# Attention heads turned by VectorE in 32x32 blocks and by transfers that exchange blocks, in place of TensorE

## What is computed

```python
for l in range(3):                       # first network, one head
    scores = leaky(si[:, :, None] + sj[:, None, :] + attn_b[l])
    attn = softmax(where(mask, scores, -inf))
    h = layernorm(x + attn @ x, g1[l], beta1[l])
    x = layernorm(h + gelu(h @ W1[l] + b1[l]) @ W2[l] + b2[l], g2[l], beta2[l])
x = layernorm(x0 + x)
xp = x @ W_proj                          # second network, 8 heads
scores = leaky(a_src[:, :, :, None] + a_dst[:, :, None, :] + b_att)
att = softmax(where(A > 0, scores, -1e30))
x = layernorm(x + relu(att @ xh))        # xh: xp by heads
```

## Time and profile before

| | us |
|---|---|
| median of 3 runs | 2389.0 (2386.5 to 2389.7) |
| the profiled execution | 2386.6 |
| its span, first to last instruction | 2384.8 |
| start, to the first unit | 52.4 |
| pair 0 | 241.7 |
| each pair from 2 to 6 | 281.0 |
| tail, from the last unit's first product | 176.3 |

### The profile page before, as it was taken

The page is one execution under the profiler, slowest core; times in us unless marked ns, Lnnn a source line. Parts: engine busy times, 40 slices in busy tenths (PEclk is TensorE's granted clock), DMA queues, the critical chain, the costliest instruction groups (busy, mean ns, idle before and its releaser), DMA issues.

```text
span 2384.8 us, 33626 instructions
## 1 busy us (share of the span) xinstructions
PE 2285.7 (96%) x11169; PEld 1629.3 (68%) x11169; DVE 1715.9 (72%) x5676; ACT 1775.3 (74%) x3415; POOL 168.0 (7%) x200
## 2 busy tenths in 40 slices
PE   3999999999999999999999999999999999999866
PEld 2667667767776776777677777767776776777543
DVE  5455886588767877678766787668867687767587
ACT  2444478877888778887787878887788877888786
POOL 0000100000000000000000000000100000000000
PEclk9999999999999999999999999999999999999977
DMA  6011021022111132011320121210211111200011
GB/s 214 10 36 36 33 96 61 20 67 89 44 55 49 34 105 63 22 50 37 97 72 23 67 85 27 76 50 32 93 42 54 54 36 63 67 19 23 31 44 33
DMA packets 85783, 131.56 MB, mean 55 GB/s; under 512 B 4424, under 2 KB 53868, under 8 KB 85612
## 3 DMA queue, kind: packets, MB, share of 16 engines
q1 hardware_dynamic: 85612, 129.41, 16.7%
HBM read 120.74 MB, written 8.65 MB: 54 GB/s over the span
## 4 chain that ended last, share of the span: by engine, by line
PE 86%; DVE 6%; ACT 6%; issue 1%; DMA 0%; POOL 0%; SPq 0%; POOLq 0%; DVEq 0%; ACTq 0%
PE ffn L1116 25%; PE av L1041 13%; PE ffn L1105 12%; PE av L1105 12%; PE pT L1024 12%; PE av L1057 5%; ACT prob L459 2%; PE av L1092 2%; PE av L1140 1%; PE trow L1140 1%; DVE prob L703 1%; ACT prob L453 1%; PE trow L1003 1%; DVE prob L694 1%; ACT l1x L493 1%
## 5 line engine op out<-in xcount | busy, mean ns | idle before, releaser
L1116 PE MATMUL ffn<-w_sb,G 128*128 128x256 f32 x3072 | 752.5, 381 | 0.9 <-ACT G L477 0.9
L1116 PEld LDWEIGHTS ffn<-w_sb,G 128*128 128x128 f32 x3072 | 553.5, 191 | 77.9 <-issue 14.2
L1024 PEld LDWEIGHTS pT<-ident,prob 128*128 128x128 f32 x2816 | 356.2, 145 | 207.1 <-issue 121.5
L703 DVE CUSTOM_DVE_ANT_0 prob<-trow,mask 128x512 f32<-128x512 f32 x704 | 458.3, 686 | 38.8 <-PE av L1065 16.9
L1024 PE MATMUL pT<-ident,prob 128*128 128x128 f32 x2816 | 440.1, 282 | 45.9 <-DVE prob L748 16.1
L459 ACT ACTIVATE prob<-prob,nm 128x512 f32<-128x512 f32 x512 | 362.8, 711 | 0.0
L453 ACT ACTIVATE prob<-prob,s 128x512 f32<-128x512 f32 x512 | 349.2, 714 | 9.1 <-DVE nm L710 7.7
L1105 PE MATMUL ffn<-hT,w_sb 128*128 128x512 f32 x768 | 354.9, 595 | 1.1 <-ACT hT L472 1.1
L1105 PE MATMUL av<-hT,w_sb 128*128 128x512 f32 x768 | 353.3, 592 | 0.0
L468 ACT COPY prob<-pT 128x512 f32<-128x512 f32 x452 | 260.7, 581 | 101.8 <-PE pT L1024 100.3
L409 POOL TENSOR_TENSOR rstd<-veps,mhalf 128x4 f32<-128x4 f32 x127 | 152.6, 1202 | 2175.6 <-DVE veps L638 2175.6
(11 more groups left out here) (119 smaller groups left out, 2468.2 us busy)
## 6 DMA issues: line engine op xcount, KB each, us to landing
w_sb<-in_L_gnn_W SPq DMA_DIRECT2D x48, 1024.0 KB, 8.4
trow<-rows_dram SPq DMA_DIRECT2D x128, 256.0 KB, 3.2
adj_sb<-in_adj SPq DMA_DIRECT2D x16, 1024.0 KB, 5.5
xin<-in_x SPq DMA_DIRECT2D x16, 512.0 KB, 6.3
x0r<-in_x SPq DMA_DIRECT2D x16, 512.0 KB, 4.5
out<-o SPq DMA_DIRECT2D x15, 512.0 KB, 3.0
aw_row<-in_L_gnn_attn_w SPq DMA_DIRECT2D x1, 768.0 KB
g_row<-in_L_gnn_g SPq DMA_DIRECT2D x2, 384.0 KB
```

The source lines that it names most:

```text
L703: return v.tensor_tensor_reduce(out=out_[:, t, :], in0=targets, in1=mask[:, t, :], scale=1.0, scalar=LEAST, op0=ALU.add, op1=ALU.max, accu ...
L1024: last = te.transpose(pT[bank][:, j * P:(j + 1) * P], src[:, t, j * P:(j + 1) * P], ident[:])
L1116: last = te.matmul(ffn[part][:, at:at + D], G[:, f, t * P:(t + 1) * P], w2_sb[:, g // 2 % STAGES, f, :], start=f == 0, stop=f == FT - 1)
```

## The change

Heads 0 to 101 are no longer turned by TensorE. `turn_blocks` on VectorE transposes each 32x32 block of a head in one instruction over 128 x 2048 elements, from the ring buffer into a new buffer `blocks`, of which there is one. `move` on SyncE then copies it back into the ring in 16 transfers of 32 partitions by 2 KB (64 KB each) that put each group of 32 partitions where it belongs. VectorE waits before each turn for the transfers of the head before (`s_moved`), and TensorE before `attend_heads`. The moved heads have their columns in another order, so the product reads them through a wider pattern (`sources`). Heads from 102 on (`MOVED`, unit `BY_PE` = 44) are turned as before. The room for `blocks` comes from `y_att`, now a part of `prob0`, and from one row buffer less (`ROWS` = 2); VectorE therefore waits for the normalised state before it computes scores.

The order changes with it. The slots make 3, 3, 3, 3, 3, 1 heads. Four heads are attended (`spent_by`) in k0, k2 and k5 ahead of the second product's first pieces and in k3 behind the attention. A unit's second and third old heads are turned on VectorE before and after the attention, its own first head at its end. The bias sum moves behind the attention (`plus_bias`), the end of a graph from before the attention to behind it, with GpSimd's order following; the masks move from k4 to k2 (kept) and k3 (made), those in k5 stay.

```diff
-ROWS = 3
+ROWS = 2
+BLOCK = 32
+BLOCKS = P // BLOCK
-MADE_IN_SLOT = [3, 3, 3, 3, 2, 2]
-MADE_AT_LAST = [3, 3, 3, 3, 3, 1]
+MADE_IN_SLOT = [3, 3, 3, 3, 3, 1]
+BY_PE = UNITS - 4
+SPENT_IN_SLOT = [-SIDE, None, 0, SIDE, None, 2 * SIDE]
...
+MOVED = made(BY_PE)[0]
 def turned(g):
-    return made(g - 1) if g else []
+    return made(g - 1) if g > BY_PE else []
+def spent_by(g):
+    p, k = g // SLOTS - 1, g % SLOTS
+    if g > BY_PE or SPENT_IN_SLOT[k] is None:
+        return None, False
+    four = 2 * HEADS * p + SPENT_IN_SLOT[k]
+    return (four, k != 3) if four >= 0 else (None, False)
...
-        y_att = sb("y_att", [P, T, D])
+        y_att = prob0[:, :, 0:D]
+        blocks = sb("blocks", [P, BLOCKS, N])
...
+            def move(q):
+                sp.wait_ge(s_block, q + 1)
+                for a in range(BLOCKS):
+                    for b in range(BLOCKS):
+                        sp.dma_start(ring(q)[b * BLOCK:(b + 1) * BLOCK, a, :],
+                                     blocks[a * BLOCK:(a + 1) * BLOCK, b, :]).then_inc(s_moved, 16)
...
+            def turn_blocks(q):
+                dve.wait_ge(s_exp, T * (q + 1))
+                if q:
+                    dve.wait_ge(s_moved, 16 * BLOCKS * BLOCKS * q)
+                v.transpose(blocks[:].rearrange("p b (x i) -> p x b i", i=BLOCK),
+                            ring(q)[:].rearrange("p t (j b i) -> p (t j) b i", b=BLOCKS, i=BLOCK)).then_inc(s_block, 1)
...
+            def sources(q, j):
+                if q < MOVED:
+                    return ring(q)[:].rearrange("p a (t j i) -> p j t a i", t=T, j=T)[:, j]
+                return ring(q)[:, :, j * P:(j + 1) * P]
...
+                if q < MOVED:
+                    pe.wait_ge(s_moved, 16 * BLOCKS * BLOCKS * min(q + SIDE, MOVED))
...
                 if g:
                     layer_ends(1 - s, unit_of(g - 1)[2])
+                dve.wait_ge(s_hn, c("hn"))
...
                 for q in new[:1]:
                     head_maxima(q)
-                done = ended(g)
-                if done is not None:
-                    graph_sum(done)
                 if att:
-                    if ends is not None:
-                        first_network_ends(ends)
-                    attention(s2, l2, *new[1:2])
+                    if ends is not None:
+                        first_network_sum(ends)
+                        if ends % 2 == 0:
+                            first_network_ends(ends)
+                    if spent is not None and ahead:
+                        heads_out(spent)
+                    for q in old[1:2]:
+                        turn_blocks(q)
+                    attention(s2, l2, *new[1:2])
+                    for q in old[2:]:
+                        turn_blocks(q)
+                if done is not None:
+                    graph_sum(done)
+                if ends is not None and ends % 2:
+                    first_network_ends(ends)
                 if done is not None:
                     graph_out()
+                plus_bias(s, l)
                 if att:
                     fed_forward(s, 0)
-                if k >= SLOTS - 2:
-                    keep_masks(k - SLOTS + 2)
+                if k == 2:
+                    keep_masks(0)
+                if k == 3 and p < PAIRS - 1:
+                    make_masks(0)
+                if k == SLOTS - 1:
+                    keep_masks(1)
                     if p < PAIRS - 1:
-                        make_masks(k - SLOTS + 2)
+                        make_masks(1)
                 for q in new[2:]:
                     head_made(q)
                 if four is not None:
                     heads_out(four)
+                if spent is not None and not ahead:
+                    heads_out(spent)
+                if g < BY_PE:
+                    for q in new[:1]:
+                        turn_blocks(q)
```

More of the change, by code:

```diff
@@ L205, in targets_of @@
             if graph == GRAPHS - 1:
[L206 removed]
+                return prob0[0:HEADS, 0, :]
             return ring(room(graph))[0:HEADS, DT, :]
@@ L349, in _ @@
                 last = p == PAIRS - 1
-                new = made(g)
+                new, old = made(g), made(g - 1)
                 if k == 0 and not last:
@@ L360, in _ @@
                     load_rows(q + 1)
[L361 to L364, removed]
+                if g <= BY_PE:
+                    for q in old[1:2]:
+                        move(q)
                 if k == 0 and not last:
@@ L367, in _ @@
                     load_x(2 * p + 3)
+                for q in new[1:2]:
+                    load_rows(q + 1)
+                if g <= BY_PE:
+                    for q in old[2:]:
+                        move(q)
+                if ended(g) is not None:
+                    store_out(ended(g))
                 if k == SLOTS - 2 and not last:
@@ L427, in _ @@
                     inverse_deviation(ATTENDED)
+                if ended(g) is not None:
+                    inverse_deviation(LAST)
+                if first_ends(g) is not None and first_ends(g) % 2:
+                    inverse_deviation(RESIDUAL)
             inverse_deviation(FED)
@@ L531, in _ @@
                 place, four = side_by_side(heads)
+                spent, ahead = spent_by(g)
                 att = g + 1 < UNITS
@@ L584, in _ @@
                         head_rows(four)
+                    if t == 0 and spent is not None and not ahead:
+                        head_rows(spent)
                     if t == 1 and att:
@@ L918, in _ @@
                 att = g + 1 < UNITS
-                new = made(g)
+                new, old = made(g), made(g - 1) if 0 < g <= BY_PE else []
                 four = side_by_side(turned(g))[1]
-                ends = first_ends(g)
+                spent, ahead = spent_by(g)
+                ends, done = first_ends(g), ended(g)
                 if g:
                     layer_ends(1 - s, unit_of(g - 1)[2])
+                dve.wait_ge(s_hn, c("hn"))
+                dve.sem_inc(s_passed, 1)
                 if att:
@@ L1200, in _ @@
                             turn(q, f - T)
+                if four_spent is not None and ahead:
+                    attend_heads(four_spent)
                 for t in range(T):
                     piece(t)
+                    if t == 2 and four_spent is not None and ahead:
+                        heads_back(four_spent)
                 if att:
@@ L1225, in _ @@
                         attend_heads(four)
+                    if t == 0 and four_spent is not None and not ahead:
+                        attend_heads(four_spent)
                     if t == 1 and att:
@@ L1230, in _ @@
                         heads_back(four)
+                    if t == 2 and four_spent is not None and not ahead:
+                        heads_back(four_spent)
                 if place == 2:
```

52 lines of the change are left out of this document (32 added, 20 removed).

## The result

The changed kernel takes 2542.8 us (median, 2537.6 to 2547.1) against 2388.9 us, a ratio of 1.0645 (95% interval 1.0623 to 1.0667). The forecast was 2410 us within 2345 to 2470: the sign was right, the size was not, and the range ended 73 us too low. The profiled run, 2541.4 us, has a span of 2539.6 us.

What follows compares the result with a forecast made beforehand. TensorE bounded the kernel before (86% of the chain); afterwards VectorE would end last in five of six slots. Profiled 2386.6 - 6 (walk) + 25 (clock) + 3 (moves) = 2409, median 2.4 higher: 2410 us, range 2345 to 2470.

Steps and rivals of the forecast that it cites:

- The transpose: VectorE's new turn of one head, 128x2048 float32, taken at 2.25 us, the pace of the reduction; 36 us per pair.
- the cheap-transpose rival: VectorE's turns behind the attention cost only 1.23 us each, giving back 57 us: 2342 us; chance 0.13.
- VectorE's work: VectorE's busy time per pair of graphs rises from 209 by 36 to 245 us.
- The wider access pattern: TensorE's four-head product reads the moved heads through a wider pattern, costed at nothing.
- The walk: Step-by-step timing of the pair's six units, k0 to k5, summing to 281.4 us against 280.95; -6 us over the run.
- the clock: TensorE's idle gaps before the scores lower its granted clock, 0.85 us on average for 30 units: +25 us.
- the 28 us taken from TensorE: Dropped head turns free 28.1 us of TensorE per full pair, which come back as waiting for VectorE in five of six slots.
- the 252.5 us in the text: TensorE's busy time per pair after the change: 280.6 less 28.1 us for the turns removed.
- the price of an issue: Each SyncE transfer issue costs 0.30 to 0.43 us, so a head's sixteen-transfer move takes 7.3 to 10.1 us.
- the moves are late: Rival: at 0.6 us an issue a move takes 12.8 us, VectorE waits 12 us per pair: 2480 us; chance 0.17.
- The first row of a graph in k0: SyncE's row load behind the moves in slot k0, put at 12 us against 14 needed.
- moving masks and spent heads costs nothing by itself: Relocating mask work and four-head attention between slots levels the slots and by itself costs nothing.

Runs made afterwards that it cites:

- e1: Changed kernel without its transfers: VectorE still turns the heads' blocks, nothing is exchanged between partitions, products not the reference's; 2419.0 us, ratio 1.0118.
- e3: Changed kernel with 4 transfers per head instead of 16, same bytes, blocks keep their partitions, products not the reference's; 2417.6 us, ratio 1.0123.
- e5: The kernel of e3 with TensorE's gaps filled by 16 unread identity transposes in each unit behind one that made heads; 2439.9 us, ratio 1.0219.
- e8: Kernel before with only the changed kernel's storage (two row buffers, shared attended array), no head turned by VectorE; 2394.6 us, ratio 1.0028.
- e2: Changed kernel with the same 16 transfers per head, each carrying 32 KB instead of 64 KB, products not the reference's; 2533.6 us, ratio 1.0615.
- e10: Changed kernel with each head's 16 transfers shared by two queues, 8 issued by SyncE and 8 by GpSimd; 2551.5 us, ratio 1.0686.
- e4: Changed kernel with TensorE turning every head, no VectorE transposes or transfers, new order and storage kept except the four-head products' places; 2452.6 us, ratio 1.0269.

## Why the prediction was wrong

**The steps that held.** *The transpose*: 2310 ns against 2.25 us, so the cheap-transpose rival is out by its own row. It took the reduction's pace. *VectorE's work*: 246 us per pair against 245. *The wider access pattern*: a matmul of the four-head product takes 602 ns in both kernels, 114 us in all. *The walk.* VectorE's period from one second feed-forward sum to the next, mean of pairs 2 to 6, in us:

| slot | walk | e1 | e3 | after | of it waiting for moves |
|---|---|---|---|---|---|
| k0 | 48.4 | 49.5 | 49.8 | 49.5 | 0 |
| k1 | 42.1 | 43.3 | 43.0 | 50.1 | 8.47 |
| k2 | 48.1 | 48.3 | 48.4 | 51.9 | 3.95 |
| k3 | 47.8 | 48.7 | 48.7 | 50.0 | 1.95 |
| k4 | 46.1 | 46.5 | 46.9 | 49.6 | 2.49 |
| k5 | 48.9 | 49.9 | 49.6 | 54.2 | 4.16 |
| sum | 281.4 | 286.2 | 286.4 | 305.3 | 21.02 |

With moves absent (e1) or in time (e3), the sum lies 4.8 to 5.0 us above the walk; the clock's 0.85 us in five slots is 4.3 of that. So the waiting for VectorE that eats the 28 us taken from TensorE is there as forecast. *The clock's* size fits, though no run separates it: in e3, which has nothing else to slow them, the first layer's matmuls have means of 621 and 618 ns where the kernel before had 595 and 592; 768 x (26 + 26) ns is 40 us over 48 units, 0.83 us each. A granted clock of 0.97 over the 286 us of e3's pair is an estimated 17 us at the lower level, 3.4 us in each of five slots, about as long as the forecast's gap. One such gap in the kernel after, a stretch of 4 us in which TensorE worked for 1.1 us, and the stretch behind it (columns as above):

```profile
1258.00:1262.00 4.00, 1.09 (x7) 0.84 (x7) 3.92 (x18) 0.69 (x1) 0.00 (x0) 1.00 0.42 107
1262.00:1266.00 4.00, 4.00 (x7) 1.58 (x6) 3.72 (x12) 1.42 (x3) 0.00 (x0) 0.57 0.10 25
```

Behind the gap the granted clock is 0.57, close to the lower of the two levels, as in the earlier trace rows. Whether all of its cost lies on the path stays open, since e5 did not separate it. TensorE's busy time is longer than the 252.5 us in the text, too: 264 us per pair in e1 and e3 and 270 in the kernel after. In e3's pair some 7 of the 11 us lie in the first layer's matmuls.

**The step that failed: the price of an issue, and where its waits fall.** The text put an issue at 0.30 to 0.43 us, from the earlier trace rows, and a move at 7.3 to 10.1 us. It was 0.59 us in the median, 10.0 to 11.1 us for sixteen, 11.5 to 12.9 for a move. The rows taken were those of one small store and of broadcasts out of DRAM; no row of before showed an SBUF-to-SBUF transfer, and I took the cheap end although the same rows held 1.51 us for one weight load (one issue, not several, and no row shows that the queue was full, as the rival has it). The rival "the moves are late" had exactly this size, 0.6 us and 12.8 us, and still gave 2480: it counted 12 us of waiting per pair, and there are 21. It laid waits into k2 to k5 from the 10 us between the turns on either side of the attention, and none into k1, because k1 was TensorE's slot there. The shorter distance it left out: from the third old head's turn to the turn at the unit's end. k1 has neither masks nor spent heads there, so by the walk's own terms only 1.8 + 2.9 = 4.7 us lie between the two, and in k2 7.8. In the trace, from the end of the one turn to where the wait for the next begins, it is 4.7 and 7.9, and the waits there are 7.3 and 4.0 us. A move at the text's own 10.1 us would already have waited 5.4 in k1 and 2.3 in k2, where the sum had 3 us for the whole run. k1's slack over VectorE was 1.8 us, its waits together 8.5: TensorE's slot became VectorE's, and grew by 8 us. The account closes: the forecast's 2410 held 3 us for moves, so the rest was 2407; walk and clock ran to 2419 (e1), and the moves added 124, which is 2543. Of the 12 us between 2407 and 2419, e8 suggests that 6 are the new storage, which the text put at nothing and which costs them outside the loop.

The Trainium skill, DMA: Bandwidth & Descriptors ("Measured"), gives 0.95 us for 64 KB. The estimate of 15.2 us worked out from it erred the other way: it adds a whole transfer sixteen times, where here sixteen issues in a row and one landing took 12 us. The page calls transfers under 64 KB descriptor-dominated; the trace agrees, since e2's 32 KB land in 1.9 us and the 64 KB in 2.0. The same page ("Issuing engine by pattern") calls transfers issued by SyncE generally faster than GpSimd's. In e10 the trace does not agree in the median: an issue took 496 ns on GpSimd and 592 on SyncE, with landings of 2.3 and 2.5 us. At the extremes it does: eight issues took up to 8.0 us on GpSimd, which paused between them, and up to 6.2 on SyncE, and the longest landings were 6.5 and 4.5 us.

**Smaller ones.** The first row of a graph in k0 was late, as the text's 12 us against 14 left room for: VectorE waits 1.51 us for it in the pair shown, 21.7 in the run, of which 12.4 stand in e3 too. VectorE at 88% was wrong: it is 76% of the run (80% in e3) and 80% of the pair shown, since the pair grew. That "moving masks and spent heads costs nothing by itself" no run tests alone: e4 leaves the spent heads where they were, and its loss comes from a graph's end behind the attention.

## What to carry to other kernels

A transfer between partitions is priced by its issue, one after another on its queue, so count issues before bytes; and when it frees the only buffer of an in-order engine, lay the whole move from trigger to landing against the shortest distance between two of its uses, slack slots included. An idle engine's queue is free for issues only at places where nobody soon waits for its next result. When one engine's work can go to another with less room than the work taken, move what fits into its waits and no more: 42 of 128 heads gained 2.3%, and 48 on two queues 2.5%, while 102, in their own order, lost 6.5%, and 1.2% even without any transfer (e1).

## What the runs showed of the hardware

- An SBUF-to-SBUF transfer's issue on SyncE is 591 ns in the median for 32 partitions of 1 KB as for 32 of 2 KB, and 603 for 128 of 2 KB. Broadcasts out of DRAM cost 0.34 us on the same queue.
- VectorE's block transpose of 128x2048 float32 takes 2310 ns, close to the 2279 of an int32 reduction over the same size, with 2300 to 2315 as extremes.
- A transfer's issue occupies GpSimd itself (496 ns each): 598 us busy in e10 instead of 189, and what it computes next comes later by that. In e10 eight of them took 4.2 us in the median and up to 8.0.
